# GpSimd makes three of the five product chunks of a unit, in the units between two rounds of gathers

## What is computed

```python
e = stack of 50 table lookups                     # (1024, 50, 300)
q1, q2 = _attn_pool(e, ...), _attn_pool(e, ...)   # dots, softmax, weighted sum over the 50 fields
h = concatenate([q1, q2]) @ w5 + b5               # (1024, 300)
f6 = h @ w6 + b6
iu, ju = triu_indices(300, k=1)
g = (v @ v.T)[iu, ju]
cross = h[:, iu] * h[:, ju] * g                   # 44850 products of pairs in each row
f7 = cross @ w7 + b7
out8 = concatenate([f6, f7]) @ w8 + b8
z = einsum('bu,bku->bk', out8, label_embedding)   # 200 rows of 300 for each batch row
y = relu(relu(concatenate([z, dense_ctx]) @ W_top1 + b_top1) @ W_top2 + b_top2) @ W_top3
```

## Time and profile before

| | us |
|---|---|
| median of 3 runs (1827.42 to 1828.97) | 1827.99 |
| the profiled execution | 1827.58 |
| its span, first to last instruction | 1825.8 |
| PE busy | 1686.1 |
| DVE busy | 1658.0 |
| ACT busy | 1014.6 |
| POOL busy | 576.0 |

### The profile page before, as it was taken

One profiled execution on the slowest core, in us unless ns is written; L12 is line 12 of the kernel. 1 busy time (PEld: TensorE's weight loads), 2 busy tenths in 40 slices (PEclk: granted clock), 3 DMA queues, 4 the chain that ended last, 5 costly groups with the idle time before them and its releaser, 6 DMA issues.

```text
span 1825.8 us, 25763 instructions
## 1 busy us (share of the span) xinstructions
PE 1686.1 (92%) x6990; PEld 1243.0 (68%) x6990; DVE 1658.0 (91%) x5831; ACT 1014.6 (56%) x3183; POOL 576.0 (32%) x420
## 2 busy tenths in 40 slices
PE   2888999999999999999999999999999999997755
PEld 1645667777767777777777777767776677775545
DVE  5988989989999889999999999899999888957678
ACT  3776693684357644456554674445754344354536
POOL 7777806828300044500067108700000000000027
PEclk8899999999999999999999999999999999999986
DMA  9488856857987689888878866998648999989996
GB/s 276 108 274 297 308 179 209 326 169 278 381 329 296 244 318 373 328 363 322 299 243 307 318 248 204 352 418 352 229 161 341 420 420 377 417 306 419 418 415 264
DMA packets 98221, 561.69 MB, mean 308 GB/s; under 512 B 16799, under 2 KB 17157, under 8 KB 72477
## 3 DMA queue, kind: packets, MB, share of 16 engines
q1 hardware_dynamic: 77917, 498.35, 70.8%
q0 software_dynamic: 19424, 61.65, 10.7%
q10 hardware_dynamic: 736, 0.05, 0.0%
HBM read 559.98 MB, written 0.00 MB: 307 GB/s over the span
## 4 chain that ended last, share of the span: by engine, by line
PE 44%; DVE 33%; DMA 9%; POOL 6%; issue 6%; ACT 2%; SPq 0%; DVEq 0%; POOLq 0%; ACTq 0%
PE acc L1223 38%; DVE junk L772 12%; DVE qa L820 12%; DVE prod L930 8%; DMA w_sb<-in_w 8%; POOL x L711 4%; POOL lab L711 2%; DMA lab<-in_labels 1%; ACT waste L1369 1%; PE coarse L1014 1%; PE acc L1061 1%; PE acc L1064 1%; PE misc L1026 1%; PE coarse L1118 1%; PE acc L1046 1%
## 5 line engine op out<-in xcount | busy, mean ns | idle before, releaser
L1223 PE MATMUL acc<-w_sb,prod 128*128 128x300 f32 (+2 forms) x5648 | 1510.7, 421 | 62.9 <-DMA w_sb<-in_w 35.0
L1223 PEld LDWEIGHTS acc<-w_sb,prod 128*128 128x128 f32 (+2 forms) x5648 | 1048.2, 191 | 430.4 <-issue 52.7
L1474 ACT ACTIVATE prod<-prod,g_all 128x256 f32<-128x256 f32 (+4 forms) x1615 | 675.0, 470 | 477.1 <-DVE prod L930 472.4
L711 POOL DMA_INDIRECT x<-in_tbl,ids_sb x368 | 488.4, 1327 | 644.5 <-DVE qa L820 534.2
L930 DVE TENSOR_TENSOR prod<-fine,coarse 128x1280 f32<-128x1280 f32 (+3 forms) x320 | 418.6, 1314 | 85.1 <-PE coarse L1014 69.3
L772 DVE SCALAR_TENSOR_TENSOR junk<-lab,heads 128x300 bf16<-128x300 f32 x1192 | 471.1, 459 | 12.6 <-DMA lab<-in_labels 7.7
L772 DVE SCALAR_TENSOR_TENSOR junk<-x,heads 128x300 bf16<-128x300 f32 x1112 | 439.0, 460 | 24.0 <-DMA x<-in_tbl,ids_sb 23.6
L820 DVE SCALAR_TENSOR_TENSOR qa<-x,ex,qa 128x300 f32<-128x300 f32 x612 | 275.4, 520 | 0.1
L746 POOL TENSOR_TENSOR x<-x,out 128x2400 f32<-128x2400 f32 x4 | 21.2, 5288 | 583.3 <-ACT out L1326 583.3
L1369 ACT ACTIVATE waste<-x 128x300 bf16<-128x300 f32 x368 | 161.6, 439 | 26.0 <-DMA x<-in_tbl,ids_sb 25.2
L1294 ACT ACTIVATE fine<-misc 128x512 f32<-128x512 f32 (+3 forms) x67 | 36.3, 542 | 112.3 <-PE misc L1026 83.7
(11 more groups left out here) (142 smaller groups left out, 604.2 us busy)
## 6 DMA issues: line engine op xcount, KB each, us to landing
w_sb<-in_w SPq DMA_DIRECT2D x320, 750.0 KB, 6.8
lab<-in_labels SPq DMA_DIRECT2D x144, 1200.0 KB, 8.7
x<-in_labels SPq DMA_DIRECT2D x51, 1200.0 KB, 12.0
x<-in_tbl,ids_sb POOLq DMA_INDIRECT x368, 5.5
fine<-in_labels SPq DMA_DIRECT2D x2, 1200.0 KB, 11.1
prod<-in_labels SPq DMA_DIRECT2D x2, 1200.0 KB, 13.6
w_sb<-in_w SPq DMA_DIRECT2D x5, 450.0 KB, 4.5
w_sb<-in_labels SPq DMA_DIRECT2D x1, 1200.0 KB, 12.4
```

Of the source, the lines that this page charges most:

```text
L711: pool.indirect_dma_start(out=row_of(t, n), out_offset=None, in_=tables[n], in_offset=bass.IndirectOffsetOnAxis(ap=ids_sb[:, t % IDS_RING, ...
L1223: last = pe.matmul(acc[:, t % 3, 0:EMB], prod[0:rows, u % RING, m, t % 2 * P:(t % 2 + 1) * P], w7_sb[0:rows, u % W7_RING, m * EMB:(m + 1) ...
L1474: act.activation(chunk, chunk, ACT.Copy, scale=g_all[0:rows, pair:pair + 1]).then_inc(chunk_ready, 1)
```

## The change

A set of units, `SHARED`, is worked out from the plan: for each tile t from 2 to 6, the units from the fourth one behind its last `wsums` up to the unit of the first `wsums` of tile t + 1, folded ones left out. By the functions of the diff, worked through, these are the units 62 to 72, 92 to 110, 136 to 153, 176 to 191 and 207 to 234, 91 in all, each with two tiles. In these units

- DVE copies the coarse window from PSUM to SBUF (`kept`, one buffer), once for each window, that is 48 times. Before it overwrites `kept`, it waits for all of GpSimd's earlier shares.
- `cross(u)` makes the first two chunks only.
- GpSimd makes chunks 2 to 4 with one instruction (`share_of`), from `kept` and the fine sets, when `kept` is there and PE has used unit u - 3. The shares of a set stand in its queue behind the 50 gathers of tile t + 1.
- ACT waits for the share ahead of chunk 2, and PE's `turn_coarse` also waits for the copy of the window that it overwrites.

The planner counts 9 in place of 14 for a `cross` of these units, and is run three times until the sets and the order fit each other. That moves DVE's items: the weighted sums of tile 4 start in unit 110 (before: 113), those of tile 5 run over the units 153 to 172 (before: 163 to 173), those of tile 6 from 191 to 203 (before: from 193). The slabs done when the last tile is pooled rise, and `SWITCH`, the slab from which the rows' buffer serves as slots too, is 124 in place of 112. To make room for `kept`, `JUNK` is 2 in place of 3, the constant `pads` is one column read 50 times, and `f7s` lies in `dup`. The last extra slab loads are kept behind the last w7 load (here the load of slab 182 also moves one place ahead of it), and the end's sums are counted from where they stand, which comes out as before.

```diff
-JUNK = 3
+JUNK = 2
+SHARE = 3
+POOL_CROSS = (0, 5, 9)
-                now = max(now, ended[c - RING]) + CROSS[len(active(c))]
+                now = max(now, ended[c - RING]) + (POOL_CROSS if c in pooled else CROSS)[len(active(c))]
...
+GATHERS_END = 4
+def free_of_gathers(items):
+    busy = [[u for u in range(TOTAL) for kind, of, _ in items[u] if (kind, of) == ("wsums", t)]
+            for t in range(1, TILES)]
+    until = [units[0] + 1 for units in busy[1:]] + [TOTAL]
+    return [[u for u in range(units[-1] + GATHERS_END, end) if not folded(u)]
+            for units, end in zip(busy[1:-1], until[1:-1])]
+PLAN = plan(())
+for _ in range(2):
+    PLAN = plan(frozenset(u for units in free_of_gathers(PLAN[1]) for u in units))
+AFTER_GATHERS = free_of_gathers(ITEMS)
+SHARED = frozenset(u for units in AFTER_GATHERS for u in units)
+def own_chunks(u):
+    return chunks_of(u) - SHARE * (u in SHARED)
+def keeps_window(u):
+    return u in SHARED and not (u - 1 in SHARED and window_of(u - 1) == window_of(u))
...
+            def share_of(u):
...
+                pool.wait_ge(window_kept, windows_kept(u))
+                pool.wait_ge(fine_ready, fills_before(u))
+                pool.wait_ge(unit_used, u - RING + 1)
...
+                pool.tensor_tensor(prod[0:rows, u % RING, own_chunks(u):FINE, cols],
+                                   fine_sets[0:rows, made + own_chunks(u):made + FINE, cols],
+                                   window, ALU.mult).then_inc(shared_ready, 1)
             for t in range(2, TILES):
...
                     gather(t, n)
...
+                for u in AFTER_GATHERS[t - 3] if t > 2 else ():
+                    share_of(u)
...
-                rows, chunks = rows_of(u), chunks_of(u)
+                rows, chunks = rows_of(u), own_chunks(u)
+                if keeps_window(u):
+                    if shares_up_to(u - 1):
+                        dve.wait_ge(shared_ready, shares_up_to(u - 1))
+                    dve.tensor_copy(kept[0:rows, slot * P:(slot + n) * P], window).then_inc(window_kept, 1)
...
+                        if m == own_chunks(u):
+                            act.wait_ge(shared_ready, shares_up_to(u))
```

More of the change, by code:

```diff
@@ L204, with plan @@
 FIRST_CROSS, GATHERED, FIRST_GATHER, PACE = 45, -230, 63, 75
-def plan():
+SHARE = 3
+POOL_CROSS = (0, 5, 9)
+def plan(pooled):
     before, items, tail = [], [[] for _ in range(TOTAL)], []
@@ L319, in plan, with shares_up_to, windows_kept, windows_kept_up_to @@
     return before, items, tail, pool_ticks, loads, switch
-BEFORE, ITEMS, TAIL, POOL_TICKS, LOADS, SWITCH = plan()
+GATHERS_END = 4
[8 more added lines that the diff above has]
+    PLAN = plan(frozenset(u for units in free_of_gathers(PLAN[1]) for u in units))
+BEFORE, ITEMS, TAIL, POOL_TICKS, LOADS, SWITCH = PLAN
+AFTER_GATHERS = free_of_gathers(ITEMS)
+SHARED = frozenset(u for units in AFTER_GATHERS for u in units)
+def own_chunks(u):
+    return chunks_of(u) - SHARE * (u in SHARED)
+def shares_up_to(u):
+    return sum(v in SHARED for v in range(u + 1))
+def keeps_window(u):
+    return u in SHARED and not (u - 1 in SHARED and window_of(u - 1) == window_of(u))
+def windows_kept(u):
+    return sum(keeps_window(v) for v in range(u + 1))
+def windows_kept_up_to(w):
+    return sum(keeps_window(v) for v in range(TOTAL) if window_of(v) <= w)
 LABELLED = {item[1]: u for u in range(TOTAL) for item in ITEMS[u] if item[::2] == ("slab", SLABS - 1)}
@@ L437, in order_last_loads @@
     loads.insert(loads.index(("w7", TOTAL - 1)) + 1, extra[0])
-    loads.insert(loads.index(("slab", LAST + END_SLOTS - 2)), extra[1])
-    loads.insert(loads.index(("slab", LAST + END_SLOTS - 1)) + 1, extra[2])
+    weights_end = loads.index(extra[0]) + 1
+    loads.insert(max(weights_end, loads.index(("slab", LAST + END_SLOTS - 2))), extra[1])
+    loads.insert(max(weights_end + 1, loads.index(("slab", LAST + END_SLOTS - 1)) + 1), extra[2])
     return loads
@@ L472, in dlrm_tower @@
         top3_sb = sb("top3_sb", [P, M2])
-        pads = sb("pads", [P, FIELDS])
+        pad = sb("pad", [P, 1])
+        pads = bass.AP(tensor=pad[:].tensor, offset=pad[:].offset,
+                       ap=[list(pad[:].ap[0]), [0, FIELDS]])
         g_all = sb("g_all", [P, CHUNKS])
@@ L493, in dlrm_tower @@
         picked = sb("picked", [P, PICKED, 2, P])
+        kept = sb("kept", [P, 2 * P])
         prod = sb("prod", [P, RING, FINE, 2 * P])
@@ L499, in dlrm_tower @@
         big = sb("big", [P, 2 * ECN * P])
-        small = sb("small", [P, EMB])
+        small = sb("small", [P, 2 * P])
         qt = big[:, 0:QCN * P]
@@ L505, in dlrm_tower @@
         h1t = big[:, 0:M1 * P]
-        f7s = small[:, 0:EMB]
+        f7s = dup[:].rearrange("p m t b -> p (m t b)")[:, 0:EMB]
         zt = small[0:ZC, 0:ZCN * P]
@@ L572, in dlrm_tower @@
         chunk_ready = sem("chunk_ready")
+        window_kept = sem("window_kept")
+        shared_ready = sem("shared_ready")
         unit_used = sem("unit_used")
@@ L681, in _ @@
                     sp.wait_ge(cross_ready, FREE_FINE)
+                    sp.wait_ge(shared_ready, shares_up_to(FREE_FINE - 1))
                 elif n == LAST + END_SLOTS + 1:
@@ L727, in _ @@
             load_ids(2)
+            def share_of(u):
+                slot, n = slots_of(u)
+                cols = slice(slot * P, (slot + n) * P)
+                rows, made = rows_of(u), first_set(u) + (not opens(u)) * FINE
+                pool.wait_ge(window_kept, windows_kept(u))
+                pool.wait_ge(fine_ready, fills_before(u))
+                pool.wait_ge(unit_used, u - RING + 1)
+                window = kept[0:rows, cols]
+                window = bass.AP(tensor=window.tensor, offset=window.offset,
+                                 ap=[list(window.ap[0]), [0, SHARE], [1, n * P]])
+                pool.tensor_tensor(prod[0:rows, u % RING, own_chunks(u):FINE, cols],
+                                   fine_sets[0:rows, made + own_chunks(u):made + FINE, cols],
+                                   window, ALU.mult).then_inc(shared_ready, 1)
             for t in range(2, TILES):
@@ L750, in _ @@
             dve.memset(ones, 1.0).then_inc(filled, 1)
-            dve.memset(pads[:], PAD).then_inc(filled, 1)
+            dve.memset(pad[:], PAD).then_inc(filled, 1)
             for r in range(JUNK):
@@ L795, in mask @@
                 for head in range(2):
-                    dve.copy_predicated(score[:, t % 2, head, :], empty[:], pads[:]).then_inc(chain, 1)
+                    dve.copy_predicated(score[:, t % 2, head, :], empty[:], pads).then_inc(chain, 1)
                 then(t, 4)
@@ L1011, in turn_coarse @@
                     pe.wait_ge(cross_ready, last_unit(w - 2) + 1)
+                    if windows_kept_up_to(w - 2):
+                        pe.wait_ge(window_kept, windows_kept_up_to(w - 2))
                 rows = rows_of(u)
@@ L1488, in _ @@
             respond("f7s", TILES - 1, 0, 0)
+            summed = 0
             for name, of, n in END_BURSTS:
-                for summed in {"zt": range(2), "z_first": range(2, FIRST_SUMS),
-                               "z_rest": range(FIRST_SUMS, len(BY_POOL))}.get(name, ()):
-                    sum_rows(summed)
+                for slab in range(summed, {"zt": 2, "z_first": FIRST_SUMS,
+                                           "z_rest": len(BY_POOL)}.get(name, summed)):
+                    sum_rows(slab)
+                    summed = slab + 1
                 respond(name, of, n, TILES % 3)
```

## The result

The changed kernel takes 1851.62 us (median of 4 runs, 1850.35 to 1853.37), the kernel before 1828.13 on the same chip: a ratio of 1.0135 [1.0123, 1.0147]. The forecast of 1847, slower, lies 4.6 us under it. The profiled execution took 1850.35 us with a span of 1848.5. The rule shares 91 units with 48 copies in this build: 62 to 72, 92 to 110, 136 to 153, 176 to 191 and 207 to 234.

A forecast was written before the change was run, and what follows sets the result against it. PE was taken as the bound in the middle, with DVE full mostly of filler; 1827.6 + 21.8 (wait) + 2.5 (clock) + 3 (unit 207) - 8 (relief) = 1846.9, so 1847 us, range 1831 to 1858.

The forecast's parts named there:

- The wait at unit 62: At the first shared unit, PE stands still 21.8 us because the share waits behind tile 3's last gather.
- The clock: Behind the stall at unit 62, a lowered PE clock costs 2.5 us, range 1.7 to 3.4.
- The pieces of the change: In shared units: DVE crosses of 0.68 us, copies of 0.42, GpSimd shares of 1.7 to 2.2; DVE gains 53 us.
- Rival D: In shared units, DVE stands still while GpSimd multiplies, 1.7 us each: 91 us atop the stall, 1940; chance 0.04.
- The relief: In three middle stages, lighter DVE returns PE's idle time: 8 us, from nothing to 9.9 and perhaps 4 more.
- One of my own signs of being wrong: Forecast is wrong if DVE's new order of work starves PE where it did not before; no size given.
- The end: In the tail, one slab less saves DVE 3.1 us, but DVE waits 9.5 us for out8 there: nothing.
- The other sets: No wait near units 92, 136 and 176; a short one near unit 207, 3 us, from 0 to 12.
- The figure for the old order: At unit 207, the old order of DVE's work would make PE wait 16 us for late gathers of tile 7.
- Rival A: Sets of tile 6 or 7 are late too, by up to 16 us in place of 3: 1862; chance 0.12.
- C: After unit 62's stall, later small waits vanish, up to 14 us together with DVE's lighter load: 1835; chance 0.14.

The follow-up runs named there:

- e1_late_set: Changed kernel with the first shared set cut to units 68 to 72 in place of 62 to 72; 1830.14 us, ratio 1.0016 to the kernel before.
- e4: Changed kernel with the shares of units 62 to 66 placed among the last 20 gathers of tile 3, one behind every fourth; 1832.49 us, ratio 1.0034.
- e8: Changed kernel with the first shared set cut to units 65 to 72; 1833.89 us, ratio 1.004 to the kernel before.
- e6_old_order: Kernel before's order of items and loads, with 89 units shared in sets beginning only where gathers are out; 1814.56 us, ratio 0.9937.
- e2: Changed kernel with the planner's new order but no share and no copy; 1859.26 us, ratio 1.0183 to the kernel before.
- e5: e1_late_set with the kernel before's load order from the w7 load of unit 286 on; 1827.40 us, ratio 1.0004.
- e9: e6_old_order with sets beginning where the change's rule puts them (62, 92, 136, 177, 207; 105 units); 1865.98 us, ratio 1.021.
- e1_again: e1_late_set timed once more, unchanged, beside other kernels on the same chip; 1832.03 us, ratio 1.0032 to the kernel before.

## Why the prediction was right, and where its terms were off

**The wait at unit 62: right.** Forecast 21.8 us, measured 21.86; ACT waited 22.6 and DVE 20.9, and DVE was held after one set of rows (the earlier trace rows gave it). The pieces are off by a tenth or two each and cancel: the share began 0.10 us behind the last gather (forecast 0.3) and took 1.81 (1.7). That nothing before unit 62 is changed holds for the order of the work, not for the buffers, as said above; gathers and PE were early by the same 3 us, so the wait is not touched by it. It is shown by leaving out six units (e1_late_set), by moving the shares within the queue (e4) and by a later beginning (e8).

**The clock: 1.8 us in place of 2.5.** The first 16 records after the wait take 373 ns each, those before it 260 (6.23 / 24), and 0.373 - 0.260 = 0.11 us by 16 is 1.8. Windows of PE alone show the granted clock in the wait and in three pieces behind it (length, busy time and count, granted clock, DMA share, GB/s):

```profile
353.20:375.06 21.86, 0.00 (x1) 0.61 0.51 153
375.06:377.00 1.94, 1.94 (x4) 0.50 0.00 0
377.00:379.00 2.00, 2.00 (x6) 0.64 0.00 0
379.00:381.00 2.00, 2.00 (x11) 1.00 0.02 3
```

PE stands still and the clock falls; it is at its lower level (1.2 GHz, the 0.50) when the work comes, and back at 1.00 from 379 on. From 379.7 to 660 it is 1.00, so no more than these records was slow. The 1.8 us are the low end of the range that I gave.

**The pieces of the change: right.** The groups by shape have these rows (count, busy us, mean ns):

```profile
L845 DVE SCALAR_TENSOR_TENSOR junk<-lab,heads 128x300 bf16<-128x300 f32 x1256 | 496.3, 460 | 11.1 <-DMA lab<-in_labels 10.2 <-issue 0.4 <-PE misc L1151 0.2
L795 POOL TENSOR_TENSOR prod<-fine,kept 128x768 f32<-128x768 f32 x75 | 135.6, 1822 | 278.5 <-DVE kept L1004 247.6 <-PE acc L1302 21.5 <-ACT fine L1373 9.3
...
L1007 DVE TENSOR_TENSOR prod<-fine,coarse 128x512 f32<-128x512 f32 x75 | 50.9, 679 | 8.4 <-PE acc L1302 8.4
...
L1004 DVE COPY kept<-coarse 128x256 f32<-128x256 f32 x39 | 16.4, 421 | 29.8 <-POOL prod L795 20.9 <-PE coarse L1093 8.8
```

Cross 679 ns (forecast 0.68), copy 421 (0.42), share 1822 (1.7 to 2.2). DVE's 52 us less busy time is my 73 - 20 = 53. With 1822 ns for 768 elements and 5288 for 2400, GpSimd takes 2.12 ns an element and 0.19 us fixed; the forecast's 2.20 had the fixed part in it.

**Rival D is out.** DVE's 1256 label rows lie between 447 and 468 ns, with 460 as the mean, whether a share runs beside them or not. The rule of the Trainium skill (SBUF — State Buffer, section "Who interferes with whom"), that a DVE instruction with a single SBUF input leaves GpSimd alone, agrees with this: the cross and the rows read their other operand from PSUM.

**The relief: near as a net sum, wrong in its parts.** I took 8 us, PE's idle time in three stages, less 3 at unit 207; the changed kernel gains 5.7 up to unit 250. But with the order held still the shares give 14.3 there and 12.3 at the end (e6_old_order). That is a little over my upper end of 9.9 and 4, since the stretches between my three stages gain as well, 3.7 us between units 113 and 176 alone: PE's small waits for ACT's chunks sum to 19.1 us in place of 26.6, and the same records are busy for less. The new order takes the difference away. I priced the relief as if the order of the work stood still. One of my own signs of being wrong, that the new order starves PE where it did not before, came true in part: between 113 and 176 the changed kernel loses 2.7 us where the old order with shares gains 3.7. Without its shares the new order costs 32 us (e2), so most of what they give in it goes to pay for it.

**The end: this step failed; forecast at nothing, it costs 8.1 us.** I looked at the number of slabs in the tail, not at the order of loads ahead of them. Three parts can be told apart. Ahead of units 318, 321 and 324 slab loads stand before w7 loads: 3.0 us from unit 312 on, shown by e5 and by the other traces. Between 284 and 312 some 1.7 are lost, of which the old order with shares loses 1.0 too. Between 250 and 284 another 3.4 are lost, where the old order with shares loses 0.8. The windows of e1_late_set show that DVE is out of work there, and one of the kernel before stands under them, each of 40 us:

```profile
1540.00:1580.00 40.00, 37.54 (x151) 27.63 (x150) 29.98 (x106) 17.95 (x44) 0.00 (x0) 1.00 1.01 415
1580.00:1620.00 40.00, 39.60 (x169) 29.88 (x170) 9.23 (x8) 15.24 (x43) 0.00 (x0) 1.00 0.46 159
```

```profile
1580.00:1620.00 40.00, 40.00 (x172) 30.15 (x171) 21.58 (x74) 15.24 (x44) 0.00 (x0) 1.00 0.87 347
```

From 1580 to 1620 the DMA engines are 46% busy in place of 87 and DVE works for 9 us in place of 22, while just before PE had idled for 2.5 us with the DMA engines full. DVE has done its label rows early and has drawn the slabs early, so loads of w7 stood behind them, and then both had nothing to do. That the early slabs are what delays w7 here is read from these windows and was not tried by itself.

**The other sets: nearly nothing, right.** Units 92, 136 and 176 have no stall. At unit 207 I forecast 3 us; PE waits for ACT there in two pieces of half a microsecond:

```profile
1191.04 1.25 PE L1302 MATMUL acc<-w_sb,prod 128*128 128x300 f32 x4 [0.52 <-ACT prod L1555]
...
1194.06 1.28 PE L1302 MATMUL acc<-w_sb,prod 128*128 128x300 f32 x4 [0.54 <-ACT prod L1555]
```

The figure for the old order, 16 us at unit 207, and about 14 at the set of tile 6 that I expected in e9, are 13.75 and 12.81 of wait in that kernel. Rival A would have been right there, and is out here because the sums of tiles 5 and 6 come earlier.

**C, a stall made good,** did not happen to any size: the closest comparison is the same order with the late first set. From unit 63 to 324 that kernel falls 5.2 us behind the kernel before (e1_late_set) or 3.1 (e1_again), the changed one 2.4. So at most 0.7 to 2.8 us of some 24 are caught up behind the stall, and six more shared units lie in the same stretch. C's own sum was off as well: its text allows 14 us and its sum takes off 16; with 14 it is 1837.

**Why the sum was near.** Against the forecast of +19.3 the profiled execution shows +22.8: 0.1 more for the wait, 0.7 less for the clock, 0.7 more of net relief, 8.1 more at the end and 3.2 less from the start-up. The sign and the 22 us are understood; that the end and the start-up, which I had both at nothing, partly cancel is luck.

**What stays open.** With late sets the new order is 1832.0 - 1814.6 = 17.5 us behind the old one. In the traces of e1_again and e6_old_order 3.0 us of it are the last loads. The rest is spread: 3.4 us between units 63 and 113, 6.4 between 113 and 176, 3.0 between 250 and 284, 0.7 between 176 and 214, and the execution of e6_old_order comes to unit 62 by 1.9 us earlier. The sets differ a little too, 85 units against 89. No run separates these.

## What to carry to other kernels

Work moved to an idle engine starts when that engine's queue comes to it, not when its operands are ready: count what stands ahead in the queue (here 18 gathers at 1.25 us), compare the time with the wish of the engine that is the bound, and begin the set later or put the work among the others. When a list scheduler is told new costs, it changes things that the edit does not speak of, and the right comparison is the new work in the old order. Here, with each set begun when its gathers are out, that was faster by 12 us, where the changed kernel was slower by 23; with the sets begun by the rule it was slower by 39. Ask for the relief and for the order separately, but do not add them: each is worth something else with the other than without it. Check the loads behind the changed stage too.

## What the runs showed of the hardware

Going from indirect DMAs to multiplications and back costs GpSimd's queue nothing that shows: 0.10 us lie between gather and share at 372.55 and 0.15 between share and gather in e4, where two gathers stand 0.30 apart. Ahead of the very first share stand two short instructions on its sequencer:

```profile
L795 POOL TENSOR_TENSOR prod<-fine,kept x91: 1808/1823/1840, 372.6 to 1337.2; 128x768 f32<-128x768 f32 x75, 126x768 f32<-126x768 f32 x16
L795 POOLq MODIFY_POOL_CONFIG  x2: 37/37/37, 372.5 to 372.6; - x2
```

The first multiplication is no dearer than the others: 1.81 us. The Trainium skill (GPSIMD Engine Reference, section on instruction dispatch) states some 6 us of code loading for the first call of a freshly loaded kernel, 5.95 measured; nothing of this kind lies ahead of this share.
